# Cumulative sums of the slot exponentials from two rounded parts, two steps later in the turn

## What is computed

```python
s = clip(hs @ Ws1.T @ Ws2.T + bs2, -32, 32)      # slot scores, per head and token
z = cumlogsumexp(s, axis=time)
es = exp(s); enz = exp(-z)                       # enz = 1 / cumsum(es)
A = where(causal, (q @ k.T) * DK**-0.5, 0)
ok = enz * (A @ es)
qv = softmax(ok)
W2 = where(causal, (qv * enz) @ es.T, 0)
o = W2 @ v
out = (rms_norm(o) * w * silu(g)) @ Wo.T
```

## Time and profile before

| | us |
|---|---|
| median of three runs | 1765.73 (1761.0 to 1766.4) |
| the profiled execution | 1762.23 |
| its span, first to last instruction | 1760.4 |
| PE busy in the span | 1624.6 |
| DVE busy | 1283.4 |
| ACT busy | 840.4 |
| POOL busy | 554.6 |
| mean granted TensorE clock | 0.976 of full speed |

### The profile page before, as it was taken

The page is one execution under the profiler, slowest core; times in us unless marked ns, Lnnn a source line. Parts: engine busy times, 40 slices in busy tenths (PEclk is TensorE's granted clock), DMA queues, the critical chain, the costliest instruction groups (busy, mean ns, idle before and its releaser), DMA issues.

```text
span 1760.4 us, 51382 instructions
## 1 busy us (share of the span) xinstructions
PE 1624.6 (92%) x21686; PEld 1145.0 (65%) x21686; DVE 1283.4 (73%) x2850; ACT 840.4 (48%) x1372; POOL 554.6 (32%) x949
## 2 busy tenths in 40 slices
PE   6999999999958899998999888998998899999989
PEld 5899999999743455554566555665454466666657
DVE  8877787788586888878898352443467798988954
ACT  3433433433441566556567712442243376776752
POOL 5454544534251222403302031541112123431230
PEclk9999999999988999999999979999999999999999
DMA  4010100110026553352462383562913036764200
GB/s 132 1 49 1 49 13 15 65 33 1 21 74 115 101 140 59 100 102 38 102 122 50 72 325 121 190 206 106 163 37 66 20 65 133 133 106 77 42 2 25
DMA packets 91856, 143.93 MB, mean 82 GB/s; under 512 B 14870, under 2 KB 60123, under 8 KB 91628
## 3 DMA queue, kind: packets, MB, share of 16 engines
q1 hardware_dynamic: 87228, 127.79, 31.6%
q10 hardware_dynamic: 2528, 7.74, 1.3%
q0 software_dynamic: 1872, 5.13, 0.8%
HBM read 109.68 MB, written 32.03 MB: 81 GB/s over the span
## 4 chain that ended last, share of the span: by engine, by line
PE 75%; DVE 14%; issue 4%; ACT 4%; POOL 1%; DMA 1%; another core or an unknown queue 1%; ACTq 0%; SPq 0%; POOLq 0%; DVEq 0%
PE bank L1002 22%; PE bank L1210 8%; PE bank L1959 5%; PE bank L1845 4%; PE bank L1847 4%; PE bank L1846 4%; PE bank L740 3%; PE bank L1978 3%; DVE xa_part_max L1283 3%; PE bank L2406 2%; PE bank L677 2%; DVE shared L1283 2%; PE bank L2421 1%; ACT xa_e L1244 1%; PE bank L704 1%
## 5 line engine op out<-in xcount | busy, mean ns | idle before, releaser
L1283 DVE TENSOR_REDUCE xa_part_max<-bank 128x1 f32<-128x448 f32 (+1 forms) x512 | 266.3, 568 | 22.3 <-PE bank L1002 19.5
L1244 ACT ACTIVATE xa_e<-bank 128x1024 f32<-128x1024 f32 (+1 forms) x208 | 211.7, 1023 | 107.5 <-PE bank L1002 105.9
L1244 ACT ACTIVATE ca_e<-bank 128x1024 f32<-128x1024 f32 (+2 forms) x208 | 197.8, 958 | 75.5 <-PE bank L1002 74.5
L1283 DVE TENSOR_REDUCE shared<-bank 128x1 f32<-128x400 f32 (+1 forms) x384 | 205.5, 570 | 21.3 <-PE bank L1002 18.0
L1002 PE MATMUL bank<-xa_kst,xa_qst 122*32 122x448 bf16 (+1 forms) x2048 | 177.5, 345 | 16.1 <-DVE xa_part_max L1283 7.7
L1210 PE MATMUL bank<-xa_e,xa_vaug 128*17 128x256 f32 (+1 forms) x1664 | 132.2, 383 | 4.7 <-ACT xa_e L1244 2.5
L1002 PE MATMUL bank<-xa_qst,xa_kst 128*32 128x256 bf16 (+1 forms) x3264 | 134.1, 274 | 0.0
L1210 PE MATMUL bank<-ca_e,ca_vaug 128*17 128x256 f32 (+2 forms) x1664 | 124.1, 365 | 7.0 <-issue 4.5
L938 POOL TENSOR_TENSOR gsa_qk<-gsa_qk,gsa_rot 128x512 f32<-128x512 f32 x64 | 81.8, 1278 | 138.1 <-DVE gsa_rot L856 138.1
L1002 PE MATMUL bank<-xa_wkv,shared 128*32 128x256 f32 (+1 forms) x1632 | 111.1, 393 | 5.6 <-DVE xa_r L1659 2.5
L1002 PEld LDWEIGHTS bank<-xa_qst,xa_kst 128*32 128x32 bf16 (+1 forms) x3264 | 92.9, 97 | 30.5 <-issue 3.0
(11 more groups left out here) (406 smaller groups left out, 4149.2 us busy)
## 6 DMA issues: line engine op xcount, KB each, us to landing
xa_kst<-xa_k_parts SPq DMA_DIRECT2D x96, 200.1 KB, 5.6
ca_kst<-ca_k_parts SPq DMA_DIRECT2D x96, 200.1 KB, 5.2
xa_k_parts<-xa_parts SPq DMA_DIRECT2D x24, 400.2 KB, 4.8
ca_k_parts<-moe_ctx_parts SPq DMA_DIRECT2D x8, 1200.8 KB
moe_gu<-in_expert_gate_up SPq DMA_DIRECT2D x8, 1024.0 KB
shared<-in_ctxT_split ACTq DMA_DIRECT2D x4, 1601.0 KB, 9.2
moe_ctxT<-in_ctxT SPq DMA_DIRECT2D x8, 800.5 KB, 8.0
ca_cv<-in_ctx SPq DMA_DIRECT2D x4, 1536.0 KB
```

What stands on the lines that cost most here:

```text
L1244: e.activation(self.e[m % 3][0:rows, :, first:T], banks[m % 2][0:rows].rearrange("p a (h t) -> p (a h) t", t=T)[:, :, first:T], ACT.Exp, s ...
L1283: e.tensor_reduce(top, work[:, 0:hi - lo], AX.X, ALU.max).then_inc(*reduced(t, *step))
```

## The change

From unit 4 on (`SPLIT_SUMS = B`, and B is 4), the sums are made from two parts of the exponential: `es_hi`, the exponential rounded to float32r, and `es_rest`, the difference `es - es_hi`, rounded too. ACT makes `es_hi` by a second exponential ahead of the first; a new step `es_rest`, on POOL, makes the difference. PE then runs six float32r matmuls of 256 columns instead of three in fp32. The matmuls of `ok` and the turning of `es` still read `es`. Units 0 to 3 stay as they are. The triangle and the ones are loaded into a part of `shared` and copied to `causal` by ACT, as float32r, in `es` 0. In a turn `cs` moves from before `a` s and `o` p to behind them; in `last_turns` it moves behind the second `gate`.

```diff
-        qz_all = sb("qz", [P, 4, T])
-        qz = [qz_all[:, i] for i in range(2)]
+        qz = [sb(f"qz{i}", [P, T])[:] for i in range(2)]
+        es_hi = sb("es_hi", [P, TB, GM])
...
+        es_rest = sb("es_rest", [P, TB, GM])
...
+        es_rested, SPLIT_SUMS = local("gsa", "es_rest"), B
...
-                    ("scale", m - 3, 1), ("ot", m - 3, 0), ("qk", s + 2), ("gate", p + 1), ("w2", p),
-                    ("ok", s - 1), ("ot", m - 3, 1), ("cs", m), ("a", s), ("o", p),
+                    ("scale", m - 3, 1), ("ot", m - 3, 0), ("qk", s + 2), ("es_rest", m), ("gate", p + 1), ("w2", p),
+                    ("ok", s - 1), ("ot", m - 3, 1), ("a", s), ("o", p), ("cs", m),
...
-                    ("qk", 61), ("z", 26), ("gate", 26), ("z", 27), ("cs", 15), ("gate", 27), ("ot", 12, 0), ...
+                    ("qk", 61), ("es_rest", 15), ("z", 26), ("gate", 26), ("z", 27), ("gate", 27), ("cs", 15), ("ot", 12, 0), ...
...
-            e.dma_start(causal[:], const("causal")[:, 0:2 * P]).then_inc(...)
+            e.dma_start(shared[:, 4 * D:4 * D + 2 * P], const("causal")[:, 0:2 * P]).then_inc(...)
...
                 elif kind == "cs":
+                    if n < SPLIT_SUMS:
...
+                    parts = [es_hi[:].bitcast(F32R), es_rest[:].bitcast(F32R)]
+                    c_, o_ = causal[:, 0:P].bitcast(F32R), ones.bitcast(F32R)
+                    q.wait_ge(es_rested, n)
+                    for i, p in enumerate(parts):
+                        e.matmul(ps[:, 0:GM], c_, p[:, 0, :], start=(i == 0), stop=(i == 1))
+                    for i, p in enumerate(parts):
+                        e.matmul(ps[:, GM:2 * GM], o_, p[:, 0, :], start=(i == 0), stop=False)
+                        m = e.matmul(ps[:, GM:2 * GM], c_, p[:, 1, :], start=False, stop=(i == 1))
+                    m.then_inc(*cs_mm(n))
...
                 elif kind == "es":                      # ACT
                     q.wait_ge(clipped, *step)
+                    if n == 0:
+                        q.wait_ge(gsa_in["causal"], "gsa")
+                        e.copy(causal[:].bitcast(F32R), shared[:, 4 * D:4 * D + 2 * P])
+                    if n >= SPLIT_SUMS:
+                        q.wait_ge(cs_mm, n - 1)
+                        e.activation(es_hi[:].bitcast(F32R), es[n % 2][:], ACT.Exp)
                     e.activation(es[n % 2][:], es[n % 2][:], ACT.Exp).then_inc(*es_ready(n))
...
+                elif kind == "es_rest":                 # POOL
+                    q.wait_ge(es_ready, n)
+                    q.wait_ge(cs_mm, n - 1)
+                    e.tensor_tensor(es_rest[:].bitcast(F32R), es[n % 2][:], es_hi[:], ALU.subtract).then_inc(*es_rested(n))
```

More of the change, by code:

```diff
@@ L603, in gsa_loads @@
             e.dma_start(sin[:], const("sin")).then_inc(*gsa_in["rope"]("gsa", by=16))
-            e.dma_start(causal[:], const("causal")[:, 0:2 * P]).then_inc(*gsa_in["causal"]("gsa", by=16))
+            e.dma_start(shared[:, 4 * D:4 * D + 2 * P], const("causal")[:, 0:2 * P]).then_inc(*gsa_in["causal"]("gsa", by=16))
             load_wo(0)
@@ L645, in gsa_pe @@
                 elif kind == "cs":
[L646 to L651, removed]
+                    if n < SPLIT_SUMS:
+                        eb = es[n % 2]
+                        q.wait_ge(es_ready, n)
+                        e.matmul(ps[:, 0:GM], causal[:, 0:P], eb[:, 0, :], start=True, stop=True)
+                        e.matmul(ps[:, GM:2 * GM], ones, eb[:, 0, :], start=True, stop=False)
+                        e.matmul(ps[:, GM:2 * GM], causal[:, 0:P], eb[:, 1, :], start=False, stop=True).then_inc(*cs_mm(n))
+                        continue
+                    parts = [es_hi[:].bitcast(F32R), es_rest[:].bitcast(F32R)]
[7 more added lines that the diff above has]
+                    m.then_inc(*cs_mm(n))
                 elif kind == "et":
@@ L941, in gsa_pool @@
                     seen(aT[n % 2]).then_inc(*a_ready(n))
+                elif kind == "es_rest":
+                    q.wait_ge(es_ready, n)
+                    q.wait_ge(cs_mm, n - 1)
+                    e.tensor_tensor(es_rest[:].bitcast(F32R), es[n % 2][:], es_hi[:], ALU.subtract).then_inc(*es_rested(n))
                 elif kind == "sm_exp":
```

## The result

| | before | after |
|---|---|---|
| median, us | 1765.47 (4 runs, 1761.0 to 1766.4) | 1793.35 (4 runs, 1788.8 to 1801.2) |
| ratio to before | | 1.0162 [1.0141, 1.0184] |
| profiled execution, us | 1762.2 | 1790.25 |
| its span, us | 1760.4 | 1788.5 |
| mean granted clock | 0.976 | 0.973 |

The change makes the kernel 1.6% slower. I had forecast slower, by 16 us; it is 28 us, and 1793.4 lies outside my range of 1771 to 1789. The spans of the two profiled executions differ by 28.1 us, so one trace set against the other can account for it.

What follows compares the result with a forecast made beforehand. PE's issue order was taken to bound the first stage, then the ring through DVE: ten turns 14.0, n = 4 0.3, sums 0.6, last turn 2.6, causal 0.2, together +17.7 us; median 1781.5, range 1771 to 1789.

Steps and rivals of the forecast that it cites:

- the price of the sums: PE, each turn: six rounded matmuls take 0.72 us instead of 1.30 for three in fp32, 0.58 less.
- rival (e): PE's sums: rounded matmuls with this stationary tile run at fp32's 0.43 us each, +30 us; chance 0.02.
- POOL's place: `es_rest` ahead of the `w2T` selects: PE stands 1.2 us before `o`; by POOL alone a turn is 0.6 us longer.
- (b): Rival: PE's saving of 0.58 x 12 = 7.0 us comes through, the kernel is faster, near 1758 us; chance 0.06.
- (c): Rival: POOL's loss and PE's gain even out, the time stays the same, 1764 us; chance 0.04.
- the ring through DVE: DVE, POOL's add, rest and select, PE's `o`, ACT's square, DVE: 30.1 us a turn, +1.4 from DVE's idle time.
- Rival (a): Only POOL's place costs, DVE regains its 0.8 us a turn: +9.4 us, about 1773; chance 0.13.
- the last turn's hole: Turn n = 15: PE's sums wait for `es_rest` behind POOL's add, `ot` starts at 434.95 instead of 432.32: +2.6 us.
- The copy of `causal` (0.2): ACT's copy ahead of the first exponential at 27.92 us: costs between 0 and 0.4 us, taken as 0.2.
- so my sum has nothing for it: SBUF port shared by DVE and POOL: beside `es_rest` DVE has only gate p+1, reading one SBUF tile; no cost.
- Rival (d): Shared port: `es_rest` slips beside two-input DVE operations, 1.2 us in eleven turns more, +30, 1794 us; chance 0.03.
- the shift passes on: After 440 us: engines keep their order and no transfer set the pace, so the first stage's delay reaches the end.

Runs made afterwards that it cites:

- experiment 9: Changed kernel with `es_hi` copied behind the tanh, `es_rest` earlier on POOL, `cs` in its old places, first weights' part behind `w2`: 1753.19 us, 0.9985 to before.
- experiment 1: Changed kernel with `es_rest` moved behind the `w2T` selects on POOL in every turn: 1778.62 us, 1.0076 to the kernel before.
- experiment 10: Kernel before with only the triangle's other landing place, its copy by ACT and the new tiles, no sums split: 1755.75 us, 1.0001 to before.
- experiment 3: Changed kernel with POOL's split of `wk` moved behind `wo` and `o` p+1: 1788.26 us, 1.0154 to the kernel before.
- experiment 5: Kernel before with only `cs` moved to its new places, sums still in fp32: 1771.61 us, 1.0044 to the kernel before.
- experiment 4: Changed kernel with the last turn's `es_rest` moved ahead of `qk` 61: 1787.89 us, 1.0137 to the kernel before.
- experiment 11: Changed kernel with both the `wk` split late and the last `es_rest` ahead of `qk` 61: 1777.42 us, 1.0119 to the kernel before.
- experiment 2: Changed kernel with `cs` back ahead of `a` and `o` in the turns, last turn left as changed: 1794.64 us, 1.0195 to the kernel before.

## Why the prediction came out as it did

**Right, to 0.2 us: the price of the sums.** For 6 x 0.12 = 0.72 the traces show 0.89 in the change and 0.79 in experiment 9, the first matmul with 0.20 instead of 0.12; rival (e) is out.

**Right: POOL's place.** `o` was to start 1.2 us later than PE could; the hole is 1.39, and experiment 1 shows 1.24 us a turn for that one place. Rivals (b) and (c) fell with it.

**Right: the ring through DVE.** Turns of 30.1 us were forecast and are 30.08; idle 1.7 before the gate (1.70) and 4.5 before the reduce (4.73: the steps from the rotation by way of `o` and its square to the reduce each ran a few hundredths later than reckoned); the wait before the reciprocal gone. DVE's holes grew by 1.5 us a turn and not by 1.4, and its busy time in unit 9's turn, reckoned as unchanged, is 0.2 less (23.10 before, 22.91 after), as its records overlap more; so a part of the match is luck. Ten turns: 14.0 forecast, 14.0 measured, without the collisions. Rival (a) fell: DVE regained none of its time.

**Right: the last turn's hole.** +2.6 forecast from 432.32, +22.6 - 20.0 = 2.6 measured. **The copy of `causal` (0.2)** was a delay of ACT's queue; what it did was to move POOL's split clear of DVE's `h`, 0.7 us the other way (experiment 10). That the start shows +0.6 is chance of this execution.

**Wrong: "so my sum has nothing for it".** The step on the shared port looked only at what lies beside the new `es_rest`. The rule was named, and it did decide something, at a place that the step didn't look at: the reciprocal's move makes DVE later at L886 in every turn, and in two turns POOL's split of `wk` gets there 0.12 to 0.13 us earlier. 2.0 us each, 4.0 in all; experiment 3 shows it by moving the split, experiment 5 by having it with no `es_rest`. Rival (d) priced the same mechanism at +30, with a collision in every turn: the wrong size, and the wrong operation. That its 1794 us is the measured time is luck.

**Wrong: the last turn's term, 2.6, ended with the hole.** What comes behind it runs at 0.60 and 0.50 granted clock for 7 us: 3.2 more. I never asked what a hole of 2.9 us does to PE's clock, as the trace before had shown 1.00 from 120 to 440 us. The 3.2 is what this execution lost. Five traces with such a hole lost half of 6.8, 6.8, 3.4, 3.4 and 0 us, that is 0 to 3.4 us, and four with one of 1.0 nothing (experiment 4). What decides between them stays open.

**Wrong: "the shift passes on", and with it the range.** The order of the work passes on, but 2.3 us were added behind 510 us; in experiment 11 it is 1.3 between the traces and 4.6 between the medians. The clock is not the same in those stages: read by stretch (510 to 740, 740 to 1140, and on to the end), it is 0.94, 0.96 and 0.99 before and 0.92, 0.97 and 0.98 after. It also varies from run to run of one kernel, whose times spread by some 10 us. Whether the change moves that part or chance does is **open**: no run here tells it apart. The range's upper end, 1789, had room for 0.3 us more a turn and a few us besides, and not for the 9.5 of mechanisms that strike in single places.

In sum: 17.7 forecast; +4.0 collisions, +3.2 clock, +0.5 in turn 4 and its sums, +0.4 at the start, +2.3 behind the stage: 28.1. Of these the 4.0 is shown by experiments. The 3.2, the 2.3 and the start are read from one execution, and other executions have them otherwise.

## What to carry to other kernels

What an operation costs is decided by its place: the same 1.26 us on POOL cost 1.24 a turn ahead of the selects and nothing where POOL had been waiting. When a step is moved, list for each engine what arrives later, and hold every VectorE operation with two SBUF inputs against every GpSimd operation that may be running when it starts, not only against the new ones. And price a new hole in PE twice: what it takes itself, and what the clock behind it may take (0 to 3.4 us here), as a range.

## What the hardware did that I had not expected

- A shift of some tenths of a microsecond turned a VectorE operation of 0.69 us into one of 2.82: the GpSimd operation of 2.40 had started 0.13 us earlier. In the other order, with the split starting as DVE's operation ended, neither took longer.
- Behind a hole of 2.91 us the granted clock fell to 0.50 for 6.8 us, but the same kind of hole (2.88 to 2.91) in four other kernels was followed by 6.8, 3.4, 3.4 and 0 us of it. Behind the holes of 1.63 to 1.70 in experiment 2 it fell to 0.50 for 3.4 us in five of eleven cases. Behind the change's own holes in the turns, eleven of 1.4 us and two of 1.7, it stayed at 1.00, and behind those of 1.0 too. PE was busy without a break while it was low, and each time it came back.
- VectorE's `h` (L355), with one tensor in SBUF as input, took 2.57 us where it started 0.06 ahead of a GpSimd operation of 2.36, and 0.52 where it started 0.32 ahead.
- Six float32r matmuls of 256 columns start 0.12 us apart, where fp32 ones took 0.43 each; splitting a sum in two rounded parts therefore costs PE less than the sum in fp32 (0.79 to 0.89 for 1.30).
